# Adding the near half of the position bias to the row-maximum search by matmuls instead of in VectorE's reduction

## The chip, the cores and the metric

The kernel runs on one core of a Trainium2 chip. The metric is the device time of one execution, in microseconds (us). TensorE is called PE below, VectorE DVE, ScalarE ACT, GpSimd POOL, and SyncE, which here only issues DMAs, SP.

## The reference, cut to what matters

Two transformer-like layers run one after the other on an input of 2 x 2048 rows of 256 numbers. The change touches only the first stage, causal attention with 16 heads of 16 columns. For each head, with q and k from one projection of x:

```
s[i, j] = q[i] . k[j] / 16 + bias(i - j)      for j <= i  (rpb: 1023 relative positions)
p       = softmax(s[i, :])
out[i]  = p @ v
```

The bias depends on the distance alone. The table is stored less its last value, so at the distances beyond one end of it there is nothing to add. For a query in tile I, a value is added to the keys of tiles 0 to I - 8 (`FAR = 8`) alone. What matters here: the softmax needs the maximum of each row of s before the exponentials, and so the bias has to be in the scores from which that maximum is taken.

## The kernel before, in words

The whole program is a sequence of phases with a barrier between them. The first one, `phase_attention`, lasts from the start to about 1037 us of the profile; after it come the projection, a mixture of branches, a state-space scan and a mixture of experts, none of which is edited.

A "pair" p is one head for both batch rows b = 0, 1. Batch row 0 lives on partitions 0 to 48 and batch row 1 on 64 to 112 of the arrays `qs` and `ks` (49 rows: one row for the maximum, then 48 rows of high and low parts of q or k). So a matmul of one batch row uses the upper 64 rows of the PE array and one of the other batch row the lower 64.

Attention is a software pipeline over pairs. While pair p is scored, pair p+1 is searched for its row maxima. The loop `for p in range(-1, PAIRS + 1)` on PE has 10 steps (`STEPS`) of 4 slots x (`SLOTS`); p = -1 only searches, next to the last products of the input projection, and the passes for p = 0 to 14 do both. In each slot:

- `score` (L519) computes a piece of transposed scores of pair p, keys on the partitions, up to 512 columns; `add_far` (L535) adds a bias from the tables `far` to those pieces that need it, 12 matmuls of 64x64 tiles for both batch rows. ACT takes the exponential (L619).
- `search` (L506) computes a piece (I, g) of pair p+1, queries of tile I on the partitions, keys of group g (512 columns) along the free side. DVE takes its maximum in `largest`: a plain reduction (L714) where nothing has to be added, an add-and-maximum with a triangular mask on the diagonal (L717), and an add-and-maximum with the bias table `near` where `is_near(I, g)` (L711). An add-and-maximum issues a second instruction that reads the accumulator. 12 of the 40 pieces of a pair are near ones; all 12 stand in even slots, and all are 512 columns wide.
- `sums` (L562), in slots 1 and 3 between the two batch rows, multiplies the probabilities of the step before with v: 8 matmuls.

Three PSUM banks (`RING = 3`) hold the searched pieces and three the scored ones. A search waits until DVE has read the piece three turns before it (`S1_FREE`, semaphore `s1_read`), a score until ACT has read the piece three turns before it (`s2_read`). DVE waits for `s1_ready`.

The maxima go back into the scores as one more row of `qs`: DVE collects them (`collect`), PE transposes them (`turn_max`, L571, in slot 2 of step 0 and of step 7), DVE negates them into `mxT` (L731), and SP stores them with a DMA (`store_max`, L331) into rows 0 and 64 of `qs`. PE waits for that DMA (`mrow_loaded`) at steps 0 and 2 of the pair. POOL, in order, does `cut` (L430, the causal mask on probabilities), `gather_values` (L417) and `round_stack` (L409).

Of the kernel before, what the change touches and what calls it, by code (L numbers as in the profile page):

```python
# [123 lines left out]
REACH = FAR * P  # L124
SPAN = REACH - P + 4 * P
# [68 lines left out]
def is_near(I, g):  # L194

    return (I - FAR + 1) * P > g * CH


def hidden_turns():

    at = sorted(at for turn, at in S1_AT.items() if turn[0] == "max" and (SEARCHED[turn[2]][1] == SEARCHED[turn[2]][0] // TPC or is_near(*SEARCHED[turn[2]])))
    return {a: n % 4 for n, a in enumerate(at)}, {a: at[n - 4] + 1 if n >= 4 else 0 for n, a in enumerate(at)}
# [9 lines left out]
def phase_attention(nc, t):  # L212
# [3 lines left out]
    with nc.cleanup_on_exit(), ExitStack() as ctx:  # L216
# [4 lines left out]
        near = [sp.sb(f"near{s}", [P, SPAN], BF16) for s in range(2)]  # L221
# [5 lines left out]
        mxT = [sp.sb(f"mxT{n}", [2 * HALF, P], F32R) for n in range(2)]  # L227
# [18 lines left out]
        mrow_loaded = [sp.sem(f"mrow_loaded{n}") for n in range(2)]  # L246
        vst_ready = sp.sem("vst_ready")
# [39 lines left out]
        def _(eng):  # L287
# [28 lines left out]
            def load_near(h):  # L316
                if h >= 2:
                    eng.wait_ge(s1_read, last_search(h - 2, 0))
                at = t.tables[1, ds(h, 1), 0:1]
                eng.dma_start(near[h % 2][:, SPAN - REACH:], bass.AP(tensor=at.tensor, offset=at.offset, ap=[[1, P], [1, REACH]])).then_inc(near_loaded[h % 2], 16)  # L320

# [6 lines left out]
            def store_max(p, n):  # L328
                eng.wait_ge(s1_read, S1_AT["row", p, n] + 1)
                for b in range(2):  # L330
                    eng.dma_start(qs[p % 3][b * P // 2:b * P // 2 + 1, n * S // 2:(n + 1) * S // 2].bitcast(F32),  # L331
                                  mxT[n][b * HALF:(b + 1) * HALF, :].bitcast(F32)).then_inc(mrow_loaded[n], 16)
# [62 lines left out]
        def _(eng):  # L395
# [3 lines left out]
            for s in range(2):  # L399
# [3 lines left out]
                step(nc.gpsimd.memset(near[s][:, 0:SPAN - REACH], 0.0))  # L403
# [8 lines left out]
            def gather_values(p):  # L412
# [32 lines left out]
            for n, (kind, u) in enumerate(USES):  # L445
# [4 lines left out]
                if n == len(USES) - 10:  # L450
                    round_stack(1)
            gather_values(0)
            for p in range(PAIRS):
                for step in range(STEPS):
                    if step == 1 and p + 1 < PAIRS:
                        gather_values(p + 1)
                    if step == 3 and p + 2 < PAIRS:
                        round_stack(p + 2)
                    cut(p, step)

        @block.tensor
        def _(eng):
# [35 lines left out]
            eng.wait_ge(pool_set, 11)  # L498

            def search(p, x, b):  # L500

                I, g = SEARCHED[x]
                lo, hi = g * CH, min(g * CH + CH, (I + 1) * P)
                at = S1_AT["max", p, x, b]
                after(eng, s1_read, S1_FREE[at])
                mm = nc.tensor.matmul(s1[:, S1_BANK[at], 0:hi - lo], qs[p % 3][half(b, ROWS), I * P:(I + 1) * P],  # L506
                                      ks[p % 3][half(b, ROWS), lo:hi], start=True, stop=True)
                mm.then_inc(s1_ready, 1)
# [72 lines left out]
            for p in range(-1, PAIRS + 1):  # L581
                if p + 1 < PAIRS:
                    eng.wait_ge(stack_ready, 2 * p + 4)
                for step in range(STEPS):
                    if 0 <= p < PAIRS and step in (0, 2):
                        eng.wait_ge(mrow_loaded[1 - step // 2], 32 * (p + 1))
                        eng.wait_ge(far_loaded[p % 2], 96 * (p // 2 + 1))
                    for x in range(SLOTS):
                        for b in range(2):
# [4 lines left out]
                            if b == 0 and x in (1, 3) and p >= 0:  # L594
                                if step > 0 and p < PAIRS:
                                    sums(p, step - 1, x // 2)
                                if step == 0 and p > 0:
                                    sums(p - 1, STEPS - 1, x // 2)
                        if p == -1 and x % 2 == 1:
# [73 lines left out]
        def _(eng):  # L673
# [27 lines left out]
            def largest(p, x, b):  # L701
# [5 lines left out]
                if is_near(I, g):  # L707
                    begin = SPAN - CH - (TB - 1 - I) * P - g * CH
                    eng.wait_ge(near_loaded[p % 2], 16 * (p // 2 + 1))
                    after(eng, s1_read, HID_FREE[at])  # L710
                    nc.vector.tensor_tensor_reduce(out=hid[HID[at]][:, 0:width], in0=piece, in1=near[p % 2][:, begin:begin + width][:, ::-1], scale=1.0, scalar=-3.0e38,  # L711
# [2250 lines left out]
```

## Time and profile before

| | us |
|---|---|
| median of 3 runs | 2526.55 |
| lowest and highest | 2526.16, 2528.66 |
| profiled execution, its own time | 2526.16 |
| profiled execution, its span from first to last instruction | 2524.2 |
| PE busy over the span | 2377.9 |
| DVE busy | 1928.0 |
| ACT busy | 1434.8 |
| POOL busy | 1045.9 |

The mean granted TensorE clock is 0.981 of full speed. Busy time of PE is to be read with care: matmuls overlap, their ends are modelled, and two matmuls of different row halves of the array can run at once. Better is the distance between starts in the timeline. PE rows of the timeline merge neighbours of one line: "x2" with its start is the start of the first. "PEld" is the loading of weights. In the shapes, "49*128 49x512" is a weight of 49 rows and 128 columns with 512 streamed columns.

### The profile page before, as it was taken

What the parts mean: (1) busy time and instruction counts of PE and PEld (TensorE: products, weight loads), DVE (VectorE), ACT (ScalarE), POOL (GpSimd) and SP (SyncE); (2) the same over time, 40 slices, a digit from 0 to 9 for tenths busy, and PEclk for the clock granted to TensorE, in tenths of its full rate; (3) what the DMA queues carried; (4) which work ended last, traced back from release to release, by engine and by line L of the source; (5) the groups of instructions that cost most, each with busy time, mean ns of one, the idle gap of its engine ahead of it and who ended that gap; (6) DMA issues with size and microseconds to landing.
All of it is one profiled execution on the core that took longest, in us unless ns stands there. A gap on an engine that the chain in (4) does not pass through costs nothing. (4 is left out here: it accounts for less than half of the span.)

```text
span 2524.2 us, 42210 instructions
## 1 busy us (share of the span) xinstructions
PE 2377.9 (94%) x14291; PEld 1515.4 (60%) x14291; DVE 1928.0 (76%) x4358; ACT 1434.8 (57%) x2608; POOL 1045.9 (41%) x1030
## 2 busy tenths in 40 slices
PE   8999999999999999899999997999999999999992
PEld 4433333333333333467777775888888777787782
DVE  3888888888888884266666665999999999898366
ACT  3466666666666667444444454666566686654420
POOL 3511211111121111110000001899999887898464
PEclk9999999999999999999999998999999999999996
DMA  8644433333334421100000000111111122124694
GB/s 252 182 74 73 87 62 61 61 61 61 61 61 74 72 67 70 56 17 17 17 17 17 18 26 30 51 60 54 63 59 56 65 101 84 63 72 142 222 330 158
DMA packets 117325, 200.20 MB, mean 79 GB/s; under 512 B 16644, under 2 KB 75064, under 8 KB 113912
## 3 DMA queue, kind: packets, MB, share of 16 engines
q1 hardware_dynamic: 89880, 160.28, 24.2%
q10 hardware_dynamic: 21088, 20.45, 2.4%
q0 software_dynamic: 6144, 16.79, 2.0%
q8 instruction: 115, 1.88, 0.3%
q14 instruction: 98, 0.80, 0.1%
HBM read 114.18 MB, written 78.79 MB: 76 GB/s over the span
## 5 line engine op out<-in xcount | busy, mean ns | idle before, releaser
L619 ACT ACTIVATE ssm_in_dt<-att_s 128x512 f32<-128x512 f32 (+3 forms) x1280 | 609.9, 535 | 301.6 <-PE att_s L519 176.9
L519 PE MATMUL att_s<-att_qs,att_ks 49*128 49x512 f32 (+3 forms) x1280 | 428.8, 417 | 22.7 <-ACT ssm_in_dt L619 20.3
L519 PEld LDWEIGHTS att_s<-att_qs,att_ks 49*128 49x128 f32 x1280 | 207.5, 185 | 391.5 <-ACT ssm_in_dt L619 324.9
L506 PE MATMUL att_s<-att_ks,att_qs 49*128 49x512 f32 (+3 forms) x1280 | 427.3, 420 | 4.0 <-DVE att_qs L698 4.0
L1932 PE MATMUL ssm_ps<-ssm_hi,ssm_halves 128*128 128x512 f32 x1024 | 407.3, 398 | 14.4 <-DVE ssm_lo L2390 7.1
L1933 PE MATMUL ssm_ps<-ssm_lo,ssm_halves 128*128 128x512 f32 x1024 | 401.4, 392 | 0.0
L1934 PE MATMUL ssm_ps<-ssm_hi,ssm_halves 128*128 128x512 f32 x1024 | 401.2, 392 | 0.0
L430 POOL TENSOR_SCALAR_AFFINE_SELECT ssm_in_dt<-ssm_in_dt 128x256 f32<-128x256 f32 x256 | 104.6, 408 | 673.1 <-ACT ssm_in_dt L619 583.7
L2323 POOL TENSOR_TENSOR ssm_cc<-ssm_cc,ssm_h 128x512 f32<-128x512 f32 x256 | 332.3, 1298 | 75.8 <-DVE ssm_h L2419 67.4
L562 PE MATMUL att_o_ps<-ssm_in_dt,att_vst 128*32 128x512 f32 (+3 forms) x2560 | 340.6, 542 | 5.3 <-ACT ssm_in_dt L619 5.3
L2332 POOL TENSOR_TENSOR ssm_out_z<-ssm_out_z,ssm_cc 128x512 f32<-128x512 f32 x256 | 338.7, 1323 | 0.1
L714 DVE TENSOR_REDUCE att_partmax<-att_s 128x1 f32<-128x512 f32 x384 | 256.1, 686 | 69.5 <-PE att_s L506 67.3
L717 DVE CUSTOM_DVE_ANT_0 att_hid<-att_s,att_hidden 128x512 bf16<-128x512 f32 (+3 forms) x512 | 238.8, 488 | 85.4 <-PE att_s L506 84.5
L2116 ACT ACTIVATE ssm_cc<-ssm_ps,ssm_par 128x512 f32<-128x512 f32 x256 | 198.5, 775 | 156.1 <-PE ssm_ps L1934 155.8
L711 DVE CUSTOM_DVE_ANT_0 att_hid<-att_s,att_near 128x512 bf16<-128x512 f32 x384 | 248.8, 685 | 7.0 <-PE att_s L506 6.6
L2110 ACT ACTIVATE ssm_ps<-ssm_in_dt,ssm_par 128x512 f32<-128x512 f32 x256 | 177.1, 692 | 118.4 <-DVE ssm_h L2419 116.1
L1932 PEld LDWEIGHTS ssm_ps<-ssm_hi,ssm_halves 128*128 128x128 f32 x1024 | 193.7, 189 | 60.7 <-issue 10.2
L2395 DVE SCALAR_TENSOR_TENSOR ssm_inp<-ssm_ps,ssm_par,ssm_in_u 128x512 f32<-128x512 f32 x256 | 190.0, 742 | 41.5 <-PE ssm_ps L1934 41.4
L506 PEld LDWEIGHTS att_s<-att_ks,att_qs 49*128 49x128 f32 x1280 | 203.4, 185 | 27.4 <-DVE att_partmax L717 6.3
L1934 PEld LDWEIGHTS ssm_ps<-ssm_hi,ssm_halves 128*128 128x128 f32 x1024 | 193.9, 189 | 41.5
L1933 PEld LDWEIGHTS ssm_ps<-ssm_lo,ssm_halves 128*128 128x128 f32 x1024 | 193.9, 189 | 40.2 <-issue 1.2
L2419 DVE TENSOR_TENSOR_SCAN ssm_h<-ssm_ps,ssm_h,ssm_inp 128x512 f32<-128x512 f32 x160 | 203.0, 1269 | 0.4
(331 smaller groups left out, 3683.6 us busy)
## 6 DMA issues: line engine op xcount, KB each, us to landing
qk_halves<-ssm_in_dt SPq DMA_DIRECT2D x64, 256.0 KB, 3.0
scan_halves<-ssm_halves SPq DMA_DIRECT2D x32, 512.0 KB, 2.9
ssm_halves<-scan_halves SPq DMA_DIRECT2D x32, 512.0 KB, 3.4
moe_sorted<-att_hidden SPq DMA_DIRECT2D x31, 512.0 KB, 10.2
moe_answers<-ssm_cc ACTq DMA_DIRECT2D x62, 256.0 KB, 3.8
att_far<-bias_tables SPq DMA_DIRECT2D x96, 136.0 KB, 8.6
att_stage_q<-qk_halves SPq DMA_DIRECT2D x96, 128.0 KB, 4.4
att_stage_k<-qk_halves SPq DMA_DIRECT2D x96, 128.0 KB, 5.9
```

Source lines behind the costliest of these rows:

```text
L506: mm = nc.tensor.matmul(s1[:, S1_BANK[at], 0:hi - lo], qs[p % 3][half(b, ROWS), I * P:(I + 1) * P], ks[p % 3][half(b, ROWS), lo:hi], start ...
L519: mm = nc.tensor.matmul(s2[:, turn % RING, 0:hi - lo], ks[p % 3][half(b, ROWS), J * P:(J + 1) * P], qs[p % 3][half(b, ROWS), lo:hi], start ...
L562: mm = nc.tensor.matmul(o_ps[32 * g:32 * g + 32, b, lo:CH], vst[p % 2][b][:, J, :], prob[:, b, step % 2, x * CH + lo:(x + 1) * CH], start= ...
L619: nc.scalar.activation(prob[:, b, step % 2, x * CH + lo:(x + 1) * CH], s2[:, turn % RING, 0:CH - lo], ACT.Exp, scale=1.0 / HD).then_inc(s2 ...
L711: nc.vector.tensor_tensor_reduce(out=hid[HID[at]][:, 0:width], in0=piece, in1=near[p % 2][:, begin:begin + width][:, ::-1], scale=1.0, sca ...
L714: nc.vector.tensor_reduce(most, piece, AX, ALU.max).then_inc(s1_read, 1)
L717: nc.vector.tensor_tensor_reduce(out=hid[HID[at]][:, 0:width], in0=piece, in1=hidden[:, CH - width:CH], scale=1.0, scalar=-3.0e38, op0=ALU ...
L1932: nc.tensor.matmul(out_ps, halves[m][:, 0, k, col], hi[:, slot, k], start=k == 0, stop=False)
L1933: nc.tensor.matmul(out_ps, halves[m][:, 0, k, col], lo[:, slot, k], start=False, stop=False)
L1934: mm = nc.tensor.matmul(out_ps, halves[m][:, 1, k, col], hi[:, slot, k], start=False, stop=k == KT - 1)
L2323: nc.gpsimd.tensor_tensor(at, at, h[:, g % H_RING], ALU.mult).then_inc(multiplied, 1)
L2332: nc.gpsimd.tensor_tensor(part, part, cc[:, g % Y_RING].rearrange("p (s j) -> p s j", s=2), ALU.add).then_inc(y_added, 1)
```

## The change

The near bias is no longer added by DVE. A new PE function `add_near` adds it in PSUM, after both batch rows of the slot were searched and before `add_far`: for each half s of the array's columns of a flip matrix, one matmul per batch row, 4 matmuls per near piece pair. Only the columns that have a bias, `min(hi, (I - 7) * 128) - lo`, are streamed; for the 12 near pieces of a pair and batch row these are 512 (six times), 384, 256 and 128 (twice each): 4608 columns. The semaphore `s1_ready` of such a piece now comes from its last `add_near` matmul. DVE reads the piece with the plain reduction.

The table `near` gets the layout of `far`: two DMAs per head of 64 partitions and 1088 columns, instead of one of 128 partitions and 1024 columns. PE, instead of DVE, waits for them, at the beginning of a pair.

The row of maxima takes another way: `mxT` is stored into a new tile `mrow`, and POOL copies (and rounds) it from there into `qs`, two copies of 1x1024 (`place_max`), in its step 1 (`place_max(p, 0)`) and its step 9 (`place_max(p + 1, 1)`). PE waits for the semaphore `row_ready` of the copies instead of for the DMA.

```diff
-near = [sp.sb(f"near{s}", [P, SPAN], BF16) for s in range(2)]
+mrow = sp.sb("mrow", [P, S])
+near = [sp.sb(f"near{s}", [P, WIN], BF16) for s in range(2)]
...
 def load_near(h):
     if h >= 2:
-        eng.wait_ge(s1_read, last_search(h - 2, 0))
-    at = t.tables[1, ds(h, 1), 0:1]
-    eng.dma_start(near[h % 2][:, SPAN - REACH:], bass.AP(...ap=[[1, P], [1, REACH]])).then_inc(near_loaded[h % 2], 16)
+        eng.wait_ge(s1_ready, last_search(h - 2, 0))
+    for r in range(2):
+        eng.dma_start(near[h % 2][half(r), :], window(0, h)).then_inc(near_loaded[h % 2], 16)
...
 def store_max(p, n):
     eng.wait_ge(s1_read, S1_AT["row", p, n] + 1)
+    after(eng, row_ready, 4 * p if n == 0 else 4 * p - 2)
     for b in range(2):
-        eng.dma_start(qs[p % 3][...].bitcast(F32), mxT[n][...].bitcast(F32)).then_inc(mrow_loaded[n], 16)
+        eng.dma_start(mrow[...], mxT[n][...]).then_inc(mrow_loaded[n], 16)
...
+def place_max(p, n):
+    eng.wait_ge(mrow_loaded[n], 32 * (p + 1))
+    for b in range(2):
+        row, cols = slice(b * P // 2, b * P // 2 + 1), slice(n * S // 2, (n + 1) * S // 2)
+        nc.gpsimd.tensor_copy(qs[p % 3][row, cols], mrow[row, cols]).then_inc(row_ready, 1)
+        eng.wait_ge(row_ready, 4 * p + 3 - 2 * n + b)
...
 def search(p, x, b):
     ...
-    mm = matmul(s1[...], qs[...], ks[...], start=True, stop=True)
-    mm.then_inc(s1_ready, 1)
+    mm = matmul(s1[...], qs[...], ks[...], start=True, stop=not has_near)
+    if not has_near:
+        mm.then_inc(s1_ready, 1)
+
+def add_near(p, x):
+    I, g = SEARCHED[x]
+    lo, hi = g * CH, min(g * CH + CH, (I - FAR + 1) * P)
+    for s in range(2 if hi > lo else 0):
+        at = 15 * P - I * P + lo + s * P // 2
+        for b in (1, 0):
+            mm = nc.tensor.matmul(s1[:, S1_BANK[S1_AT["max", p, x, b]], 0:hi - lo], flip_b[half(b), s],
+                                  near[p % 2][half(b), at:at + hi - lo], start=False, stop=s == 1)
+            if s == 1:
+                mm.then_inc(s1_ready, 1)
...
 for p in range(-1, PAIRS + 1):
     if p + 1 < PAIRS:
         eng.wait_ge(stack_ready, 2 * p + 4)
+        eng.wait_ge(near_loaded[(p + 1) % 2], 32 * ((p + 1) // 2 + 1))
     for step in range(STEPS):
         if 0 <= p < PAIRS and step in (0, 2):
-            eng.wait_ge(mrow_loaded[1 - step // 2], 32 * (p + 1))
+            eng.wait_ge(row_ready, 4 * p + 2 + step)
...
+            if p + 1 < PAIRS:
+                add_near(p + 1, SLOTS * step + x)
...
 # DVE, largest(p, x, b)
-    if is_near(I, g):
-        ...
-        nc.vector.tensor_tensor_reduce(out=hid[...], in0=piece, in1=near[p % 2][...][:, ::-1], ..., op0=ALU.add, op1=ALU.max, accum_out=most)
-    elif g < I // TPC:
+    if g < I // TPC:
         nc.vector.tensor_reduce(most, piece, AX, ALU.max).then_inc(s1_read, 1)
```

On PE, around slot 2 of step 0, before (L519 score, L506 search, L571 the transposition of the maxima, L562 the sums):

```order
L506 MATMUL att_s<-att_ks,att_qs 128x512 [waits att_s1_read]
L571 MATMUL att_s<-att_ident,att_mx 16x128 [waits att_s1_read,att_mx_ready]
L519 MATMUL att_s<-att_qs,att_ks 128x512 [waits att_s2_read]
L506 MATMUL att_s<-att_ks,att_qs 128x512 [waits att_s1_read]
L562 MATMUL att_o_ps<-ssm_in_dt,att_vst 32x128
```

The same place in the changed kernel (its lines are L541 score, L515 search, L527 `add_near`, L593 transposition, L584 sums):

```order
L515 MATMUL att_s<-att_ks,att_qs 128x512 [waits att_s1_read]
L527 MATMUL att_s<-att_near,att_flip_b 128x512 x4
L593 MATMUL att_s<-att_ident,att_mx 16x128 [waits att_s1_read,att_mx_ready]
L541 MATMUL att_s<-att_qs,att_ks 128x512 [waits att_s2_read]
L515 MATMUL att_s<-att_ks,att_qs 128x512 [waits att_s1_read]
L584 MATMUL att_o_ps<-ssm_in_dt,att_vst 32x128
```

Four matmuls stand between the second search of the slot and the transposition. At slot 0 of step 2, where PE now waits for `row_ready` and where a far addition (L535 before, L557 now) stands too, the changed kernel has:

```order
L541 MATMUL att_s<-att_qs,att_ks 128x512 [waits att_s2_read,att_far_loaded1,att_row_ready]
L515 MATMUL att_s<-att_ks,att_qs 128x512 [waits att_s1_read]
L541 MATMUL att_s<-att_qs,att_ks 128x512 [waits att_s2_read]
L515 MATMUL att_s<-att_ks,att_qs 128x512 [waits att_s1_read]
L527 MATMUL att_s<-att_near,att_flip_b 128x128 x4
L557 MATMUL att_s<-att_far,att_flip_b 64x512 x12
L541 MATMUL att_s<-att_qs,att_ks 128x512 [waits att_s2_read]
```

The near additions go ahead of the far ones. On POOL, in the changed kernel (L432 the causal cut, L420 the row copies, L412 the values):

```order
L432 AFFINE_SELECT ssm_in_dt<-ssm_in_dt 128x2x128 [waits att_s2_read,att_cut_done] x8
L420 CAST att_qs<-att_mrow 1x1024 [waits att_mrow_loaded1,att_cut_done]
L420 CAST att_qs<-att_mrow 1x1024 [waits att_row_ready]
L432 AFFINE_SELECT ssm_in_dt<-ssm_in_dt 128x2x128 [waits att_s2_read,att_row_ready]
L432 AFFINE_SELECT ssm_in_dt<-ssm_in_dt 128x2x128 [waits att_s2_read,att_cut_done] x3
L420 CAST att_qs<-att_mrow 1x1024 [waits att_mrow_loaded0,att_cut_done]
L420 CAST att_qs<-att_mrow 1x1024 [waits att_row_ready]
L412 COPY att_vst<-ssm_out_z 128x16x16 [waits att_summed,att_row_ready]
```

Before, the twelve cuts stood in one run, with nothing between them. Each pair of copies now waits behind the cuts ahead of it and holds up what follows.

## Rows read from the trace of the kernel before

**Rows 1.** Busy time in a stretch: PE, PEld, DVE, ACT, POOL, clock, DMA, GB/s

```profile
500.00:560.00 60.00, 57.65 (x492) 22.94 (x490) 49.02 (x153) 40.65 (x86) 11.20 (x21) 1.00 0.32 64
```

**Rows 2.** Timeline of PE, a half step with a far addition: start, length, instructions

```profile
534.41 1.06 PE L562 MATMUL att_o_ps<-ssm_in_dt,att_vst 128*32 128x256 f32 x8
535.41 0.49 PE L519 MATMUL att_s<-att_qs,att_ks 49*128 49x512 f32 x1
...
535.75 0.62 PE L519 MATMUL att_s<-att_qs,att_ks 49*128 49x512 f32 x2
535.98 0.39 PE L506 MATMUL att_s<-att_ks,att_qs 49*128 49x512 f32 x1
536.30 0.84 PE L535 MATMUL att_s<-att_far,att_flip_b 64*64 64x512 bf16 x12
537.07 0.50 PE L519 MATMUL att_s<-att_qs,att_ks 49*128 49x512 f32 x1
...
537.50 1.06 PE L562 MATMUL att_o_ps<-ssm_in_dt,att_vst 128*32 128x128 f32 x8
```

**Rows 3.** Timeline of PE, a half step without a far addition

```profile
500.04 1.06 PE L562 MATMUL att_o_ps<-ssm_in_dt,att_vst 128*32 128x512 f32 x8
...
502.22 0.49 PE L519 MATMUL att_s<-att_qs,att_ks 49*128 49x512 f32 x1 [0.22 <-ACT ssm_in_dt L619]
...
502.77 1.06 PE L562 MATMUL att_o_ps<-ssm_in_dt,att_vst 128*32 128x512 f32 x8
```

**Rows 4.** Timeline of PE, slots 2 and 3 of step 0

```profile
522.72 0.49 PE L506 MATMUL att_s<-att_ks,att_qs 49*128 49x512 f32 x1
523.33 0.27 PE L571 MATMUL att_s<-att_ident,att_mx 128*16 128x128 f32 x1
...
523.85 0.49 PE L506 MATMUL att_s<-att_ks,att_qs 49*128 49x512 f32 x1
524.27 1.06 PE L562 MATMUL att_o_ps<-ssm_in_dt,att_vst 128*32 128x128 f32 x8
```

**Rows 5.** Timeline of DVE at the same place

```profile
523.10 0.69 DVE L711 CUSTOM_DVE_ANT_0 att_hid<-att_s,att_near 128x512 bf16<-128x512 f32 x1
...
523.71 0.69 DVE L711 CUSTOM_DVE_ANT_0 att_hid<-att_s,att_near 128x512 bf16<-128x512 f32 x1
...
525.83 0.69 DVE L714 TENSOR_REDUCE att_partmax<-att_s 128x1 f32<-128x512 f32 x1 [0.64 <-PE att_s L506]
```

**Rows 6.** Timeline of PE, narrower score and search pairs

```profile
570.18 0.43 PE L519 MATMUL att_s<-att_qs,att_ks 49*128 49x256 f32 x2
570.30 0.32 PE L506 MATMUL att_s<-att_ks,att_qs 49*128 49x256 f32 x1
...
575.05 0.38 PE L519 MATMUL att_s<-att_qs,att_ks 49*128 49x128 f32 x2
575.16 0.27 PE L506 MATMUL att_s<-att_ks,att_qs 49*128 49x128 f32 x1
```

**Rows 7.** Timeline of PE in the first pass, which only searches

```profile
89.18 0.73 PE L506 MATMUL att_s<-att_ks,att_qs 49*128 49x512 f32 x4
89.84 1.98 PE L480 MATMUL att_o_ps<-ssm_in_u,ssm_in_dt 128*128 128x512 f32 x4
```

**Rows 8.** Page, part 5: the plain and the near maximum on DVE

```profile
L714 DVE TENSOR_REDUCE att_partmax<-att_s 128x1 f32<-128x512 f32 x384 | 256.1, 686 | 69.5 <-PE att_s L506 67.3
L711 DVE CUSTOM_DVE_ANT_0 att_hid<-att_s,att_near 128x512 bf16<-128x512 f32 x384 | 248.8, 685 | 7.0 <-PE att_s L506 6.6
```

**Rows 9.** Lines of instructions: reading the accumulator on DVE, loading weights on PE

```profile
L535 PEld LDWEIGHTS att_s<-att_far,att_flip_b 64*64 64x64 bf16 x2304 | 48.0, 105 | 75.8 <-issue 64.8
L711 DVE DVE_READ_ACCUMULATOR2_ANT att_partmax<- 128x1 f32 x384 | 31.9, 83 | 0.0
```

**Rows 10.** Timeline of POOL: a cast of 2048 columns

```profile
541.42 1.90 POOL L409 CAST att_qs<-att_stage_q 113x2048 fp32r<-113x2048 f32 x1
```

**Rows 11.** Timeline of SP: the stores of a pair's maxima

```profile
524.62 1.30 SPq L331 DMA_DIRECT2D att_qs<-att_mxT  x2
```

More of the change, by code:

```diff
@@ L191 @@
 S1_BANK, S1_FREE, ALONE = search_banks()
-def is_near(I, g):
-    return (I - FAR + 1) * P > g * CH
 def hidden_turns():
-    at = sorted(at for turn, at in S1_AT.items() if turn[0] == "max" and (SEARCHED[turn[2]][1] == SEARCHED[turn[2]][0] // TPC or is_near(*SEARCHED[turn[2]])))
+    at = sorted(at for turn, at in S1_AT.items() if turn[0] == "max" and SEARCHED[turn[2]][1] == SEARCHED[turn[2]][0] // TPC)
     return {a: n % 4 for n, a in enumerate(at)}, {a: at[n - 4] + 1 if n >= 4 else 0 for n, a in enumerate(at)}
@@ L226, in phase_attention @@
         mx = [sp.sb(f"mx{n}", [P, 2, HALF]) for n in range(2)]
-        mxT = [sp.sb(f"mxT{n}", [2 * HALF, P], F32R) for n in range(2)]
+        mxT = [sp.sb(f"mxT{n}", [2 * HALF, P]) for n in range(2)]
         oT = [sp.sb(f"oT{b}", [P, CH]) for b in range(2)]
@@ L402, in _ @@
                     step(nc.gpsimd.memset(vst[s][b][:, :, HD + 1:32], 0.0))
-                step(nc.gpsimd.memset(near[s][:, 0:SPAN - REACH], 0.0))
             def round_stack(p):
@@ L451, in _ @@
                     round_stack(1)
+                if n == len(USES) - 3:
+                    place_max(0, 1)
             gather_values(0)
@@ L454, in _ @@
                 for step in range(STEPS):
-                    if step == 1 and p + 1 < PAIRS:
-                        gather_values(p + 1)
+                    if step == 1:
+                        place_max(p, 0)
+                        if p + 1 < PAIRS:
+                            gather_values(p + 1)
                     if step == 3 and p + 2 < PAIRS:
                         round_stack(p + 2)
+                    if step == 9 and p + 1 < PAIRS:
+                        place_max(p + 1, 1)
                     cut(p, step)
@@ L506, in search @@
                 mm = nc.tensor.matmul(s1[:, S1_BANK[at], 0:hi - lo], qs[p % 3][half(b, ROWS), I * P:(I + 1) * P],
-                                      ks[p % 3][half(b, ROWS), lo:hi], start=True, stop=True)
-                mm.then_inc(s1_ready, 1)
+                                      ks[p % 3][half(b, ROWS), lo:hi], start=True, stop=not has_near)
+                if not has_near:
[10 more added lines that the diff above has]
+                            mm.then_inc(s1_ready, 1)
             def score(p, step, x, b):
@@ L706, in largest @@
                 piece, most = s1[:, S1_BANK[at], 0:width], partmax[:, b, I, g:g + 1]
-                if is_near(I, g):
[L708 to L711, printed above, removed]
-                                                   op0=ALU.add, op1=ALU.max, accum_out=most).then_inc(s1_read, 1)
-                elif g < I // TPC:
+                if g < I // TPC:
                     nc.vector.tensor_reduce(most, piece, AX, ALU.max).then_inc(s1_read, 1)
```

13 lines of the change are left out of this document (6 added, 7 removed).

## The prediction

> **What bounds the kernel now.** I first asked how far each engine is busy while pairs are searched and scored together. Over a stretch of 60 us in the middle PE is busy for 57.65 of 60 us, DVE for 49.02, ACT for 40.65 and POOL for 11.20, at full granted clock [rows 1]. PE is nearly full, but that number is padded by modelled ends, so I went on to the timeline of PE and took the distances between starts.
>
> In a half step with a far addition (from one `sums` to the next, 534.41 to 537.50, 3.09 us) the pieces follow each other without a recorded wait: `sums` 1.00, the first score and search pair 0.34, the next 0.23, the third 0.32, the far addition 0.77, the last pair 0.43 [rows 2]. That adds up to 3.09. A pair of a score and a search, 512 columns each, costs 0.23 and not twice that; at 2.4 GHz 512 columns alone are 0.213. So the two row halves of the array work at once and PE streams. In this kind of half step whatever is added to PE should be paid in full.
>
> A half step without a far addition lasts 2.73 us (500.04 to 502.77), and there PE has a gap of 0.22 us before a score, waiting for ACT [rows 3]. So there some added work is free. The third kind is slot 2 of step 0: the second search starts at 522.72, the transposition at 523.33, and the search after it only at 523.85, 0.14 after DVE finished with the piece of the near maximum that it had begun at 523.10 (the next begins at 523.71) [rows 4, 5]. There PE is paced by DVE for a moment.
>
> DVE itself waits: 69.5 us in front of the plain maxima and 7.0 in front of the near ones, mostly for searches on PE [rows 8]. It does not set the pace in general.
>
> **What the change takes from DVE.** 384 add-and-maximum operations of 685 ns become 384 plain ones of 686 ns, on equal shapes: 0 [rows 8]. Also 384 accumulator reads of 83 ns go, 31.9 us in all [rows 9], but I cost them at nothing: the near maxima started at 523.10 and 523.71, 0.61 apart, less than the length of one [rows 5], so the reads already lie beside the next operation, and DVE waits for PE anyway. At best that is a gain of 32 us; it returns as a rival below.
>
> **What it adds to PE.** 12 near pieces per pair, each 4 matmuls. The two of one s are for different row halves, as the score and search pair is, so I price two matmuls as one such pair, and a near piece at two of those. A pair costs 0.23 at 512 columns [rows 2], 0.12 at 256 and 0.11 at 128 [rows 6]; for 384 I take 0.17, between. So a near piece costs 0.46, 0.34, 0.24 or 0.22 us. The lower bound is the bare stream, 2 x columns / 2400: 0.43, 0.32, 0.21, 0.11.
>
> Which slots they fall in decides how much is paid. From the table of searches: eight stand in slots with a far addition (512 columns in step 2 slot 2, step 3 slot 2 and step 6 slot 0; 384 in step 5 slot 2; 256 in steps 4 and 5, slot 0; 128 in steps 2 and 3, slot 0), four in slots without one (512 in step 0 slots 0 and 2 and in step 1 slot 2; 384 in step 6 slot 2).
>
> - The eight: 3 x 0.46 + 0.34 + 2 x 0.24 + 2 x 0.22 = 2.64 us per pair from above, 2688 columns x 2 / 2400 = 2.24 from below. I take 2.5, nearer the upper end because the pair price is a measured distance.
> - Slot 2 of step 0: the near matmuls also delay DVE. Its second search starts at 522.72; 0.23 later the first near pair goes, 0.23 later the second, at 523.18. From the start of a search to the maximum that reads it there are 0.56 (the sums of 524.27 last 1.00, so the search after them starts at 525.27, and its maximum at 525.83) [rows 2, 4, 5]. So DVE starts at 523.74 instead of 523.10, and the search that waits for this piece, and the sums after it, move by 0.64. Below, 0, if DVE's lateness is caught up; I take 0.64, since that search waits for it today.
> - The other three: between 0, in the gap, and their full 0.46 + 0.46 + 0.34 = 1.26. The gap is 0.22 where it is recorded and the price 0.46 [rows 3], so I take half, 0.63.
>
> Sum per pair 2.5 + 0.64 + 0.63 = 3.77, between 2.24 and 2.64 + 0.64 + 1.26 = 4.54. Fifteen passes score and search together: 56.6 us (33.6 to 68.1).
>
> The first pass only searches. Four searches start at 89.18, products follow at 89.84 and run on [rows 7]; nothing waits there, so its 12 pieces are paid: 6 x 0.46 + 2 x 0.34 + 2 x 0.24 + 2 x 0.22 = 4.36 from above, 4608 x 2 / 2400 = 3.84 from below; I take 4.1.
>
> The Trainium skill, "TensorE: Matmul & The Clock Gate", in Part 3 (The mechanism), says that a weight load overlaps with running matmuls only where it goes to another row group. The two values of s need different weights in the same row half, so by that rule each of the 384 steps (12 x 2 x 16) would also pay a load. The rows speak against it: successive pairs, whose weights also go to the same two halves, stand 0.23 apart, 0.02 over the bare stream [rows 2]. What an exposed load would make of the time is in a rival.
>
> **What it moves.** The row of maxima takes a detour: store, then two POOL casts of 1024 columns, in order behind POOL's cuts. A cast of 2048 columns takes 1.90 [rows 10], so about 0.95 each, 1.9 together. The two stores are issued from 524.62 to 525.92 [rows 11]. PE needs the result at the first score of step 2; the sums of 534.41 are those of slot 1 of that step, behind three pairs (0.34, 0.23, 0.32) and a far addition (0.77) and one more pair, so that score is at about 532.4. Between lie 6.5 us, of which 1.9 are casts, so the landing may take 4.6. The path of step 7 to step 0 is longer. POOL is busy for only 11.20 of 60 us [rows 1], and the 3.8 per pair fit. Its next jobs, values and a cut, come about 2 us later, still before their sums. I cost it at 0; from the other side it is at worst what the third rival says. On the SP queue one load of `near` becomes two, needed a whole pair later; the row stores keep their place. PE's wait for `near` at the head of a pair costs nothing for the same reason: 0.
>
> **Sum.** 56.6 + 4.1 = 60.7 us, bounds 37.4 and 72.5. The profiled execution took 2526.16, span 2524.2; the median of the runs is 2526.55, 0.4 apart. 2526.2 + 60.7 = 2586.9: 2587 us, 2.4% slower. Its own range is 2563 to 2600.
>
> **Rivals.**
> 1. PE is less full than it seems: its ends are modelled, and the 0.34 and 0.32 of [rows 2] against 0.23 may be waits that near matmuls would fill. Then the four slots without far additions cost nothing and the eight half, 1.25 per pair, and the first pass 2: 15 x 1.25 + 2 = 21 us, 2547. For it: DVE and ACT's idle gaps. Against: the far half step adds up with no recorded wait.
> 2. The near matmuls do not pair up, or their weight loads are exposed. One after the other they cost as much again, 2 x 60.7 = 121 us: 2648. Exposed loads at the nearest row, 105 ns for 64x64 [rows 9], cost 384 x 0.105 = 40 us on top of 60.7: 2627. For it: the trace has no 64x128 bf16 matmul. Against: the 0.23.
> 3. The detour is late at step 2. If a store takes 8 us to land instead of under 4.6, because the next pair's loads are queued right behind it, PE stands 3.4 us per pair, 54 us in all: 2641.
> 4. The other side: DVE sets the pace, through the chain search, maximum, freed bank, search. Then the accumulator reads count, 384 x 0.083 = 32 us less, and PE's additions lie in its waits: 2494. It decides from the point where DVE has no idle time in front of the maxima. Rows 8 show 76.5 us of it, so I give it little.
>
> **How the numbers follow.** Forecast 0.71, rival 1 0.12, rival 2 0.10, rival 3 0.04, rival 4 0.03. The range takes the forecast's own bounds, most of rival 1 and stops short of rival 2's: 2550 to 2620. A change under 0.2% (5 us) can't be told from none here; only a corner of rival 1 lies there, 0.02. Faster is rival 4, 0.03. Slower 0.95.
>
> **What would show it.** PE: `add_near`'s second pair starts 0.21 to 0.24 after the first at 512 columns; half steps like that of [rows 2] last 3.5 instead of 3.09; the row transposition to sums in step 0 grows by about 0.6; the stretch per pair grows by 3.8. DVE: the idle time in front of its maxima grows by some 60 us, while plain maxima keep 686 ns. POOL: casts of 1x1024 near 0.95 us, done 2 us or more before the first score of step 2. The forecast is wrong if near pairs stand 0.4 or more apart, if PE waits for POOL, or if the half steps with far additions do not grow.

## The result, and the profile after

| | before | changed |
|---|---|---|
| median, us | 2527.61 (4 runs, 2526.16 to 2528.67) | 2573.09 (4 runs, 2569.24 to 2574.62) |
| profiled execution, its own time | 2526.16 | 2575.21 |
| its span | 2524.2 | 2573.5 |
| PE busy | 2377.9 | 2437.0 |
| DVE busy | 1928.0 | 1933.2 |
| POOL busy | 1045.9 | 1110.4 |

The changed kernel takes 1.018 times as long (1.0168 to 1.0192): 45.5 us more, where 60.7 was forecast. It is slower as forecast, and inside the range. In the profiled executions the difference is 49.3 us of span, and the accounts below are made against that.

The first view is the stretch of one whole pair, from the sums of step 2, slot 1, to the same sums of the next pair. The columns are those of [rows 1]. In the changed kernel:

```profile
501.93:562.52 60.59, 59.01 (x525) 23.61 (x523) 47.66 (x125) 38.50 (x82) 15.21 (x24) 1.00 0.34 64
```

The same stretch in the kernel before:

```profile
534.41:592.05 57.64, 55.52 (x476) 22.16 (x474) 47.23 (x149) 38.51 (x82) 11.12 (x20) 1.00 0.34 66
```

A pair became 2.95 us longer, at full clock in both. DVE's busy time hardly changed (47.66 against 47.23), although 24 instructions went (the accumulator reads); POOL has 4.1 more (four casts). Fifteen such pairs are 44.3 of the 49.3 us.

Next, PE's timeline in the half step with a far addition that answers to [rows 2]:

```profile
501.93 1.07 PE L584 MATMUL att_o_ps<-ssm_in_dt,att_vst 128*32 128x256 f32 x8
502.92 0.49 PE L541 MATMUL att_s<-att_qs,att_ks 49*128 49x512 f32 x1
...
503.26 0.62 PE L541 MATMUL att_s<-att_qs,att_ks 49*128 49x512 f32 x2
503.49 0.39 PE L515 MATMUL att_s<-att_ks,att_qs 49*128 49x512 f32 x1
503.73 0.61 PE L527 MATMUL att_s<-att_near,att_flip_b 64*128 64x512 bf16 x4
504.26 0.84 PE L557 MATMUL att_s<-att_far,att_flip_b 64*64 64x512 bf16 x12
505.04 0.50 PE L541 MATMUL att_s<-att_qs,att_ks 49*128 49x512 f32 x1
...
505.47 1.06 PE L584 MATMUL att_o_ps<-ssm_in_dt,att_vst 128*32 128x128 f32 x8
```

It lasts 3.54 us (501.93 to 505.47) against 3.09: 0.45 more for a near piece priced at 0.46. The distance to the far addition is larger, 0.53 (503.73 to 504.26), but the last search now has a successor at 0.24 where it had one at 0.32. The half step without a far addition, which answers to [rows 3]:

```profile
527.42 1.06 PE L584 MATMUL att_o_ps<-ssm_in_dt,att_vst 128*32 128x512 f32 x8
...
528.98 0.39 PE L515 MATMUL att_s<-att_ks,att_qs 49*128 49x512 f32 x1
529.22 0.50 PE L527 MATMUL att_s<-att_near,att_flip_b 64*128 64x384 bf16 x4
529.59 0.49 PE L541 MATMUL att_s<-att_qs,att_ks 49*128 49x512 f32 x1
...
530.15 1.07 PE L584 MATMUL att_o_ps<-ssm_in_dt,att_vst 128*32 128x512 f32 x8
```

It lasts 2.73 us (527.42 to 530.15), exactly as before, with a near piece inside whose two matmuls in one row half start 0.17 us apart, so about 0.35 in all. The reader can see how much room there was. The near piece starts 1.80 after the sums (529.22 less 527.42). Before, the last score started 2.18 after them (502.22 less 500.04) [rows 3]. So there were 0.38 us between these two starts, not the 0.22 that is recorded as idle. Even 0.38 is not the limit. In slot 0 of step 0 a piece of 512 columns, which makes the half step above 0.45 longer, stands in the same distance:

```profile
547.44 0.39 PE L515 MATMUL att_s<-att_ks,att_qs 49*128 49x512 f32 x1
547.67 0.61 PE L527 MATMUL att_s<-att_near,att_flip_b 64*128 64x512 bf16 x4
548.05 0.44 PE L541 MATMUL att_s<-att_qs,att_ks 49*128 49x384 f32 x1
```

Its half step (545.87 to 548.55) keeps its 2.68 us too. But a piece that adds nothing to its own half step can add to the next: the half step that follows the 384 columns of step 6 has no near work, and grew from 2.87 to 2.95.

Slots 2 and 3 of step 0, PE, which answer to [rows 4]:

```profile
550.13 0.50 PE L515 MATMUL att_s<-att_ks,att_qs 49*128 49x512 f32 x1
550.29 0.80 PE L527 MATMUL att_s<-att_near,att_flip_b 64*128 64x512 bf16 x4
551.02 0.28 PE L593 MATMUL att_s<-att_ident,att_mx 128*16 128x128 f32 x1
...
551.68 0.50 PE L515 MATMUL att_s<-att_ks,att_qs 49*128 49x512 f32 x1
552.11 1.07 PE L584 MATMUL att_o_ps<-ssm_in_dt,att_vst 128*32 128x128 f32 x8
```

And DVE there, which answers to [rows 5]:

```profile
550.93 1.29 DVE L733 TENSOR_REDUCE att_partmax<-att_s 128x1 f32<-128x512 f32 x2 [0.31 <-PE att_s L527]
```

From the second search of the slot to the sums are 1.98 us (550.13 to 552.11) against 1.55 before (522.72 to 524.27) [rows 4]. DVE starts its maximum 0.80 after that search; before it was 0.38 [rows 4, 5]. It now waits for L527. So the delay runs through DVE as forecast, but is 0.42, not 0.64. There are two reasons. The first stands in the first two rows: the near matmuls start 0.16 us after the search, before its 0.213 us of columns can have passed. They belong to the other batch row, in the other row half, and stream beside it; the second one of that row starts at 550.52, 0.39 after the search and not 0.46. The second reason is the larger one: from there to the maximum are 0.41 us (550.52 to 550.93), where the forecast had put in 0.56, the distance from a search to its maximum.

The first pass of the changed kernel, which answers to [rows 7], and the transpositions of maxima, first those of the changed kernel and then those of before (least, median and greatest length in ns; first and last start):

```profile
86.66 0.49 PE L515 MATMUL att_s<-att_ks,att_qs 49*128 49x512 f32 x2
86.99 0.61 PE L527 MATMUL att_s<-att_near,att_flip_b 64*128 64x512 bf16 x4
87.25 0.58 PE L515 MATMUL att_s<-att_ks,att_qs 49*128 49x512 f32 x2
87.76 1.98 PE L488 MATMUL att_o_ps<-ssm_in_u,ssm_in_dt 128*128 128x512 f32 x4
```

```profile
L593 PE MATMUL att_s<-att_ident,att_mx x32: 269/277/380, 109.3 to 1035.0; 128*16 128x128 f32 x32
```

```profile
L571 PE MATMUL att_s<-att_ident,att_mx x32: 269/269/380, 104.8 to 983.8; 128*16 128x128 f32 x32
```

The first transposition comes 4.5 us later (109.3 against 104.8): the first pass, forecast at 4.1. The last comes 51.2 later. That is 44.3 + 4.5 and 2.4 more, which arise as the first pair begins; there both kernels have a stretch of lower granted clock. The changed kernel, four microseconds with the lowest value and then the 20 us around them:

```profile
128.00:132.00 4.00, 3.96 (x18) 2.09 (x17) 2.66 (x10) 1.92 (x5) 0.00 (x0) 0.50 0.29 76
124.00:144.00 20.00, 19.50 (x127) 8.38 (x131) 12.93 (x32) 11.58 (x24) 6.39 (x12) 0.74 0.67 106
```

In the kernel before, the 20 us that hold its own low stretch:

```profile
120.00:140.00 20.00, 19.95 (x145) 8.25 (x145) 15.52 (x48) 13.13 (x28) 5.10 (x10) 0.83 0.78 120
```

A granted 0.50 is the lower of the clock's two levels, 1.2 GHz. A mean of 0.74 instead of 0.83 over 20 us is an estimated 1.8 of the 2.4 us. It is not in every execution of this kernel: a second profile of the changed kernel, unedited (below, "The changed kernel again"), has 0.83 there, its first transposition comes at 108.9, 4.1 after that of before, and 1.1 us instead of 2.4 are left over:

```profile
124.00:144.00 20.00, 19.81 (x141) 8.16 (x145) 13.65 (x33) 11.71 (x24) 6.58 (x11) 0.83 0.73 112
```

The phases after attention, which are not edited, took 2.0 us less. Together 44.3 + 4.5 + 2.4 - 2.0 = 49.2.

Last, the detour of the maxima in the changed kernel: POOL, SP, and the first score of step 2 on PE:

```profile
554.98 2.12 POOL L420 CAST att_qs<-att_mrow 1x1024 fp32r<-1x1024 f32 x2 [3.93 <-DMA att_mrow<-att_mxT]
```

```profile
552.43 1.30 SPq L327 DMA_DIRECT2D att_mrow<-att_mxT  x2
```

```profile
560.36 0.49 PE L541 MATMUL att_s<-att_qs,att_ks 49*128 49x512 f32 x1
```

POOL waits for the landing, copies until 557.10, and PE needs the row at 560.36: 3.3 us of room. The page's groups of maxima on DVE, which answer to [rows 8]:

```profile
L733 DVE TENSOR_REDUCE att_partmax<-att_s 128x1 f32<-128x512 f32 x768 | 494.2, 686 | 112.8 <-PE att_s L515 66.3
```

The 768 maxima of 512 columns keep 686 ns, and wait 112.8 us where 76.5 (69.5 + 7.0) stood before. The diagonal maxima wait 94.6 where they waited 85.4, so all of them together wait 45.5 longer.

### The profile page after: what moved, and what is told of

It is laid out like the page before. It is cut to its first block and busy times, and to the rows that moved or that the text cites. A ratio compares the mean times of both kernels' runs of the same rounds, so it can differ in the third digit from the quotient of the medians.

```text
span 2573.5 us, 43116 instructions
## 1 busy us (share of the span) xinstructions
PE 2437.0 (95%) x15059; PEld 1542.2 (60%) x15059; DVE 1933.2 (75%) x3974; ACT 1435.0 (56%) x2608; POOL 1110.4 (43%) x1092
## 5 line engine op out<-in xcount | busy, mean ns | idle before, releaser
L733 DVE TENSOR_REDUCE att_partmax<-att_s 128x1 f32<-128x512 f32 x768 | 494.2, 686 | 112.8 <-PE att_s L515 66.3
L541 PE MATMUL att_s<-att_qs,att_ks 49*128 49x512 f32 (+3 forms) x1280 | 435.8, 421 | 16.1 <-ACT ssm_in_dt L644 13.7
L515 PE MATMUL att_s<-att_ks,att_qs 49*128 49x512 f32 (+3 forms) x1280 | 435.9, 426 | 4.4 <-DVE att_qs L723 4.3
L541 PEld LDWEIGHTS att_s<-att_qs,att_ks 49*128 49x128 f32 x1280 | 208.1, 185 | 380.1 <-ACT ssm_in_dt L644 307.3
L432 POOL TENSOR_SCALAR_AFFINE_SELECT ssm_in_dt<-ssm_in_dt 128x256 f32<-128x256 f32 x256 | 104.0, 406 | 622.7 <-ACT ssm_in_dt L644 546.4
L584 PE MATMUL att_o_ps<-ssm_in_dt,att_vst 128*32 128x512 f32 (+3 forms) x2560 | 340.8, 542 | 5.3 <-ACT ssm_in_dt L644 5.3
L736 DVE CUSTOM_DVE_ANT_0 att_hid<-att_s,att_hidden 128x512 bf16<-128x512 f32 (+3 forms) x512 | 238.9, 487 | 94.6 <-PE att_s L515 93.8
L515 PEld LDWEIGHTS att_s<-att_ks,att_qs 49*128 49x128 f32 x1280 | 204.4, 186 | 28.1 <-DVE att_partmax L733 10.4
L2419 DVE SCALAR_TENSOR_TENSOR ssm_inp<-ssm_ps,ssm_inp 128x512 f32<-128x512 f32 x256 | 170.6, 666 | 0.0
```

The source lines that it names most:

```text
L541: mm = nc.tensor.matmul(s2[:, turn % RING, 0:hi - lo], ks[p % 3][half(b, ROWS), J * P:(J + 1) * P], qs[p % 3][half(b, ROWS), lo:hi], start ...
L584: mm = nc.tensor.matmul(o_ps[32 * g:32 * g + 32, b, lo:CH], vst[p % 2][b][:, J, :], prob[:, b, step % 2, x * CH + lo:(x + 1) * CH], start= ...
L733: nc.vector.tensor_reduce(most, piece, AX, ALU.max).then_inc(s1_read, 1)
```

## The experiments

Three chips were used. On the first the kernel before took 2526.89 (17 runs), on the second 2552.8 (7), on the third 2526.49 (7); so times are compared with the kernel before on the same chip, and a time that an expectation gives in us is one of the first chip. The second chip is slower only behind attention: a pair takes 60.55 us there with the four matmuls reordered, and 60.59 in the profile above, while the phases behind attention take 1508 to 1516 us there and 1482 to 1486 on the others. Slots are told as (step, slot). "A pair" below is the stretch of the first view, and the growth of a half step is the mean of eleven pairs.

**The detour undone.** Near matmuls stay, but the maxima are stored into `qs` directly and POOL copies nothing.

```diff
-    eng.dma_start(mrow[...], mxT[n][...]).then_inc(mrow_loaded[n], 16)
+    eng.dma_start(qs[p % 3][...].bitcast(F32), mxT[n][...].bitcast(F32)).then_inc(mrow_loaded[n], 16)
...
-    place_max(p, 0)
...
-    place_max(p + 1, 1)
...
-    eng.wait_ge(row_ready, 4 * p + 2 + step)
+    eng.wait_ge(mrow_loaded[1 - step // 2], 32 * (p + 1))
```

> The changed kernel, with the row of maxima stored straight into qs again and PE waiting for that store; no row copies on POOL. Theory (all of the cost is PE streaming the near matmuls): no difference from the changed kernel, 2573 us, since the copies end about 3 us before PE's first score of step 2. Rival (the detour through POOL stands on PE's path): faster than the changed kernel, by up to 3 us a pair, 2530 to 2565.

Measured 2575.24 us (2572.07 to 2575.92), ratio 1.0189 (1.0175 to 1.0203), against 1.018 of the changed kernel. A pair takes 60.55 us against 60.59. The detour costs nothing that can be seen; the third rival is out.

**The near matmuls undone.** The detour and the plain maxima stay, `add_near` issues nothing. It leaves the near bias out of the maxima.

```diff
-    has_near = min(hi, (I - FAR + 1) * P) > lo
+    has_near = min(hi, (I - FAR + 1) * P) > lo and False
...
-    for s in range(2 if hi > lo else 0):
+    for s in range(2 if hi > lo and False else 0):
```

> The changed kernel without its near matmuls: the near bias is left out of the search, DVE reduces the pieces plainly, the detour of the maxima through POOL stays. Theory: the time of the kernel before, 2527.6 us, within 3. Rival (DVE's lost accumulator reads are a gain that the matmuls hide): 2496 to 2520. Rival (the detour costs): 2535 or more.

Measured 2523.14 (2522.23 to 2526.04, 11 runs), ratio 0.9987 (0.9978 to 0.9996), 3.7 us under the kernel before, where at most 3 were expected. The half step of [rows 2] is back at 3.09 us (535.77 to 538.86):

```profile
535.77 1.06 PE L584 MATMUL att_o_ps<-ssm_in_dt,att_vst 128*32 128x256 f32 x8
...
537.65 0.84 PE L557 MATMUL att_s<-att_far,att_flip_b 64*64 64x512 bf16 x12
...
538.86 1.06 PE L584 MATMUL att_o_ps<-ssm_in_dt,att_vst 128*32 128x128 f32 x8
```

So the matmuls are the whole cost, some 50 us. It also tells on the fourth rival: with all accumulator reads of near pieces gone and nothing added to PE, the gain is 3.7 us and not 32. Even that is not in attention: a pair takes 57.62 us here and 57.64 before, and the last sums start at 1037.2 us in this profile and at 1035.9 in that of before. It lies in the phases after it, which are not edited, and is left open.

**Four slots, and eight slots.** The near matmuls only in the four slots without a far addition, (0,0), (0,2), (1,2), (6,2); then only in the other eight. Each leaves the near bias out of the other pieces' maxima. The edit is one condition in `search` and in `add_near`:

```diff
+    ... and x in (0, 2, 6, 26)
+    ... and x not in (0, 2, 6, 26)
```

> The changed kernel with near matmuls only in the four slots that have no far addition (step 0 slots 0 and 2, step 1 slot 2, step 6 slot 2); elsewhere the near bias is left out. The prediction's term for these slots, 1.27 us a pair, gives 15 x 1.27 + 1.8 in the first pass = 21 us, 2549. The trace of the changed kernel shows only about 0.45 a pair in the half steps next to them: 15 x 0.45 + 1.8 = 9 us, 2536 to 2538. Rival (their cost spills into later half steps, 0.3 more a pair): 2541 to 2543.

> The changed kernel with near matmuls only in the eight slots that have a far addition; in the other four the near bias is left out. Theory (PE streams there, all is paid): 15 x 2.45 + 2.7 in the first pass = 39 us, 2566 to 2568, as the prediction's 2.5. Rival (the two groups overlap or compensate each other): under 2560.

Four slots: 2535.11 (2534.33 to 2539.26), ratio 1.0036 (1.0024 to 1.0048), 12.0 us over the kernel without near matmuls. A pair grows by 0.64 us, of it 0.41 in the half step of (0,2), 0.03 in that of (1,2), nothing in those of (0,0) and (6,2), and 0.20 as spill into the half steps behind (1,2) and (6,2), which have no near work here. The forecast had 1.27. Eight slots: 2562.44 (2562.28 to 2563.68), ratio 1.0142 (1.0126 to 1.0158), 39.3 us over it, 2.36 per pair, where 2.5 was forecast. The half steps grow by 0.44 to 0.50 for a piece of 512 columns, 0.34 for 384, 0.24 and 0.10 for the two of 256, and 0.13 for each of 128. The two groups add up: 12.0 + 39.3 = 51.3, beside 52.1 for all twelve without the detour (2575.24 less 2523.14) and some 49 with it (the ratios 1.018 and 0.9987). Most of the forecast's error is in the four slots.

**The near matmuls twice.** Each pair of a value of s is issued two times, 8 matmuls per piece. It adds the near bias twice to the scores that are searched.

```diff
-    for s in range(2 if hi > lo else 0):
+    for turn in range(4 if hi > lo else 0):
+        s = turn % 2
```

> The changed kernel with every near matmul issued twice (the near bias is added twice in the search). Theory (slots without a far addition hide the first dose in a gap that PE has only once): the second dose is paid nearly in full, 2.5 in the far slots and 1.4 to 1.6 in the other four, 4.0 us a pair, and 4.4 in the first pass: 2573 + 64 = 2637. Rival (these slots have room for more, as PE is not what paces them): as much again as the first dose, 2573 + 47 = 2620.

Measured 2664.07 (2660.19 to 2664.21), ratio 1.0428 (1.0411 to 1.0446), 111.3 us over before. In a far half step:

```profile
526.39 1.07 PE L585 MATMUL att_o_ps<-ssm_in_dt,att_vst 128*32 128x256 f32 x8
...
528.19 1.04 PE L528 MATMUL att_s<-att_near,att_flip_b 64*128 64x512 bf16 x8
529.16 0.84 PE L558 MATMUL att_s<-att_far,att_flip_b 64*64 64x512 bf16 x12
...
530.36 1.07 PE L585 MATMUL att_o_ps<-ssm_in_dt,att_vst 128*32 128x128 f32 x8
```

The expectation of 2637 is a ratio of 1.043, and held. The second dose adds 0.43 here (3.97 against 3.54). Eight matmuls of 512 columns pass in 0.97 us; one after another at 2.4 GHz they would take 1.71. Per pair the second dose costs 3.81 where the first cost 2.95. The difference is in the slots without a far addition, which pay some 1.6 for the second dose after 0.64 for the first. Their room is used once.

**The order of the four matmuls.** Both values of s for one batch row, then both for the other.

```diff
-    for s in range(2 if hi > lo else 0):
-        at = 15 * P - I * P + lo + s * P // 2
-        for b in (1, 0):
+    for b in ((1, 0) if hi > lo else ()):
+        for s in range(2):
+            at = 15 * P - I * P + lo + s * P // 2
```

> The changed kernel with the four near matmuls of a piece ordered by batch row first (both column halves of row b = 1, then both of b = 0), so that only the middle two can run side by side. Theory (two row halves of the array at once): three streams instead of two, 0.21 to 0.23 more for 512 columns, 1.2 us more a pair in the far slots and 0.2 to 0.7 in the others, 1.9 in the first pass: 2596 to 2604. Rival (near matmuls never ran side by side): 2573, as before the reordering.

Measured 2601.91 (2599.36 to 2603.7) on the second chip, ratio 1.0187 (1.017 to 1.0204). The expectation was wrong: it is a ratio of 1.027 to 1.030 (2596 to 2604 on the first chip; the 2601.91 is of the second), and the order makes no difference. The half step is 3.54 us again:

```profile
500.39 1.06 PE L584 MATMUL att_o_ps<-ssm_in_dt,att_vst 128*32 128x256 f32 x8
...
502.19 0.61 PE L527 MATMUL att_s<-att_near,att_flip_b 64*128 64x512 bf16 x4
502.73 0.84 PE L557 MATMUL att_s<-att_far,att_flip_b 64*64 64x512 bf16 x12
...
503.93 1.06 PE L584 MATMUL att_o_ps<-ssm_in_dt,att_vst 128*32 128x128 f32 x8
```

Either the four matmuls are not side by side at all and each is cheaper than thought, or each row half works through its own matmuls whatever stands between them. The starts inside the piece, which the view shows in a narrow window, already say the second: two begin at 502.19, though the second in the program is for the same row half as the first.

```profile
502.19 0.39 PE L527 MATMUL att_s<-att_near,att_flip_b 64*128 64x512 bf16 x2
```

The other two begin at 502.42. So the third of the program started beside the first, and before the second. Two more experiments, below, ask the same of the time.

**Narrow near matmuls.** At most 128 columns each, in the same count; it leaves out the near bias of the other columns in the search.

```diff
-    lo, hi = g * CH, min(g * CH + CH, (I - FAR + 1) * P)
+    lo, hi = g * CH, min(g * CH + P, (I - FAR + 1) * P)
```

> The changed kernel with every near matmul cut to 128 columns; the near bias is left out beyond them. Theory (the cost is streamed columns): 0.11 to 0.22 a piece in the far slots, 0.9 to 1.8 us a pair, 0.1 to 0.2 in the others, 2 in the first pass: 2523 + 18 to 32 = 2541 to 2555. Rival (the cost is the weight loads and the instructions, which are the same in number): above 2565.

Measured 2576.21 (2569.72 to 2582.63) on the second chip, ratio 1.0081 (1.0062 to 1.0099), 23.4 us over before. Its four runs are 13 us apart, so this is a rough number; a pair takes 58.80 us, 1.16 over before.

```profile
502.38 0.29 PE L527 MATMUL att_s<-att_near,att_flip_b 64*128 64x128 bf16 x4
502.60 0.52 PE L557 MATMUL att_s<-att_far,att_flip_b 64*64 64x256 bf16 x12
```

From the first near matmul to the far addition are 0.22 us, as priced, over 0.11 of bare columns. But the half step around it grew by only 0.13 (500.58 to 503.36, 2.78 against 2.65): a part of the 0.22 stood between the last search and the far addition before, too. In one row half the second near matmul starts 0.07 us after the first, where its columns take 0.053. So the cost goes with the columns even here.

**Near pieces moved out of slots with far additions.** In the table of searches (11,0) changes places with (12,3), and (14,0) with (14,1): two pieces with 512 near columns go to slots without a far addition, one with 384 comes back.

```diff
-            (12, 3), (13, 3), (13, 0), (12, 2),
-            (8, 0), (15, 3), (14, 0), (14, 2),
+            (11, 0), (13, 3), (13, 0), (12, 2),
+            (8, 0), (15, 3), (14, 1), (14, 2),
...
-            (11, 0), (8, 1), (14, 1), (10, 1),
+            (12, 3), (8, 1), (14, 0), (10, 1),
```

> The changed kernel with four search pieces exchanged: near piece (11, 0), 512 near columns, moves from step 6 slot 0, which has a far addition, to step 1 slot 0, which has none, and (12, 3) takes its place; near pieces (14, 0), 512, and (14, 1), 384, change places between step 2 slot 2 (far addition) and step 6 slot 2 (none). Theory: 0.45 + 0.08 us a pair less paid, nothing new in step 1, where PE waits 0.5 us for ACT: 2573 - 8 = 2565. Rival (DVE's maxima in step 1 come late and hold the freed banks): 2573 or more.

Measured 2588.56 (2587.78 to 2590.01) on the second chip, ratio 1.0138 (1.0121 to 1.0155): 35.8 us over before, 10 less than the changed kernel has on its chip. A pair takes 59.98 us, 0.61 less. The half step of step 6, slot 0, fell from 3.54 to 2.97, below the 3.10 of before. Not all of that is near work: the piece that came, (12,3), is searched with 128 columns where (11,0) has 512. It is the best version with all near matmuls, and still slower than the kernel before, so nothing here beats that.

**The changed kernel again, and near matmuls for one batch row only.** The first is the changed kernel without an edit, on the third chip. The second leaves the near bias out of the search of batch row 1.

```diff
-    for b in (1, 0):
+    for b in (0,):
```

> The changed kernel, unedited, to stand beside the next two on the same chip. Both theories: 1.018 of the kernel before.

> The changed kernel with the near matmuls of batch row b = 0 alone (two a piece instead of four); the near bias of b = 1 is left out. Theory (the two batch rows' matmuls stream side by side in the two row halves): the removed ones cost nothing, 0 to 8 us less than the changed kernel, some of it because the maxima of b = 1 start earlier. Rival (they stream one after the other and the pairing is only in the records): half of the 48 us goes, 22 to 26 us less.

Changed again: 2571.47 (2569.98 to 2575.2), ratio 1.018 (1.0163 to 1.0197). One row: 2569.12 (2566.94 to 2569.67), ratio 1.0167 (1.015 to 1.0184), 2.4 us less for half of the matmuls. The half step with a far addition shows why:

```profile
561.72 1.07 PE L584 MATMUL att_o_ps<-ssm_in_dt,att_vst 128*32 128x256 f32 x8
...
563.53 0.60 PE L527 MATMUL att_s<-att_near,att_flip_b 64*128 64x512 bf16 x2
564.06 0.84 PE L557 MATMUL att_s<-att_far,att_flip_b 64*64 64x512 bf16 x12
...
565.27 1.07 PE L584 MATMUL att_o_ps<-ssm_in_dt,att_vst 128*32 128x128 f32 x8
```

It lasts 3.55 us with two matmuls as with four. That is the direct proof that the two batch rows stream side by side: the second is free there. The 2.4 us themselves understate what one row saves. A pair takes 59.97 us against 60.55, 0.58 less (8.7 in fifteen). It is saved in three half steps: 0.40 in that of (0,2), and 0.11 and 0.08 in those behind (1,2) and (6,2), the same places and sizes as in the four slots above. Against it stands a longer stretch of low clock as the first pair begins, 0.57 over 20 us where the changed kernel again has 0.83, an estimated 5 us:

```profile
124.00:144.00 20.00, 18.71 (x83) 7.05 (x83) 10.63 (x27) 9.54 (x20) 5.81 (x11) 0.57 0.66 97
```

The mean clock of all four executions is lower too, 0.979 to 0.980 against 0.981 to 0.983. Why is not shown. Slots 2 and 3 of step 0 with one row:

```profile
549.81 0.50 PE L515 MATMUL att_s<-att_ks,att_qs 49*128 49x512 f32 x1
550.16 0.60 PE L527 MATMUL att_s<-att_near,att_flip_b 64*128 64x512 bf16 x2
...
551.41 1.06 PE L584 MATMUL att_o_ps<-ssm_in_dt,att_vst 128*32 128x128 f32 x8
```

Two matmuls take the 0.60 that four took. From the search to the sums are 1.60 us here (1.98 with both rows, 1.55 before). So the 0.41 that this slot lost came from batch row 1, whose maximum DVE takes first and which frees the bank for slot 3. It is not the price of streaming: batch row 0 still has its two matmuls there. The 0.20 of spill is gone as well.

**Twice, by batch row.** Eight matmuls as above, first four of batch row 1, then four of batch row 0.

```diff
-    for s in range(2 if hi > lo else 0):
-        for b in (1, 0):
+    for b in ((1, 0) if hi > lo else ()):
+        for turn in range(4):
+            s = turn % 2
```

> Every near matmul twice, as in the earlier doubled kernel, but ordered by batch row: four of b = 1, then four of b = 0 (the near bias is added twice in the search). Theory A (each row half works through its own matmuls and does not wait for the other half's in program order): the time of the doubled kernel, 1.043 of the kernel before. Theory B (starts keep program order): four streams of b = 1, and of b = 0 only the first beside the last of them, 7 streams instead of 4, 0.64 us more for a piece of 512 columns, about 5 us a pair, 1.07 of the kernel before.

Measured 2630.14 (2629.49 to 2634.12), ratio 1.0415 (1.0398 to 1.0433), against 1.0428 for eight in the paired order; a pair takes 64.37 us against 64.40, and the far half step 3.97 in both. Even four matmuls of one half in a row do not hold up the other half.

## Why the prediction was right, and where its sizes were off

- **PE bounds, far slots are paid in full: right.** Forecast 2.5 us per pair, measured 2.36 with the eight slots alone. The half step of [rows 2] was to last 3.5 and lasts 3.54. Only the 256 columns of step 5 came at less than their columns, 0.10, and the pieces of 128 were priced too high, 0.22 for 0.13. The first rival, which had the eight half hidden, is wrong there. It also said that the other four cost nothing, and for three of them that is nearer than the forecast.
- **Two row halves at once: right.** The whole piece adds 0.45, one batch row alone costs as much as both in a far half step, a second dose adds 0.43. The second rival needed twice this, or 0.1 us per weight load; neither is there. By the rule of the Trainium skill ("TensorE: Matmul & The Clock Gate", Part 3, The mechanism) that a load overlaps running matmuls only in another row group, the change of weights within a row half would have shown. The second dose, two more changes of weights in each half, cost 0.43 us where the columns alone take 2 x 0.213, which leaves no room for it. The same section also lets a load into the background weight buffer run ahead, which would fit; no run tells the two apart.
- **Slot 2 of step 0: right in kind, 0.41 instead of 0.64.** Two steps failed. One is "0.23 later the first near pair goes, 0.23 later the second": the near matmuls of batch row 1 do not wait for the search of batch row 0, and its second one started 0.39 after that search. The other is the 0.56 from there to the maximum, read off a search; behind a near matmul it is 0.41. The experiment with one batch row shows that this delay is the slot's whole cost.
- **"The other three": mis-sized, 0.63 instead of 0.23.** This is about half of the error: 0.40 x 15 = 6 us (slot 2 of step 0 is 0.23 x 15 = 3.5, the far slots 0.14 x 15 = 2.1). The step was "The gap is 0.22 where it is recorded and the price 0.46, so I take half". Read by distances between starts the gap was 0.38, and pieces of 0.35 and of 0.45 both passed in it without making their half step longer. The range had 0 as its lower bound, which was nearer. Of what was paid, 0.03 in the half step of (1,2) and 0.20 behind, the 0.20 goes away with the near matmuls of batch row 1 while those of row 0 stream on. So it is not streaming; that it comes by way of later maxima, as in (0,2), was not traced. That the room holds one dose and not two is shown by the doubled kernel.
- **First pass: right.** 4.5 in this profile, 0.1 above its upper bound of 4.36, and 4.1, as forecast, in the second profile of the same kernel.
- **The detour: right, 0.** The casts are longer than forecast, 1.03 instead of 0.95 each (a row of 1024 columns on one partition took no less per column than one on 113), and the room is 3.3 us.
- **DVE's part: right, 0.** Plain maxima are as long as the near ones were, and the reads lay beside other work; without near matmuls the kernel gains 3.7 us and not 32. DVE's idle time was to grow by 60 us, the forecast's whole cost. It grew by 36 in front of the plain and near maxima and by 9 in front of the diagonal ones, 45.5 in all, most of the 51 by which attention got longer: DVE has the same work in more time. The fourth rival's chain (search, maximum, freed bank, search) exists, but only (0,2) shows it, where it is what costs.
- **What was not in the sum:** 2.4 us more at the start of the first pair, an estimated 1.8 of them by the lower clock and not seen again in the second profile, and 2.0 less in later phases. They nearly cancel, and that is luck.

## What to carry to other kernels

Work that moves from an engine with idle time to the one that has none is paid at its full streaming price, however cheap it looks there. Recorded idle time tells too little of what would be free: it was 0.22 where the starts left 0.38, and a piece that costs 0.45 elsewhere passed there. Leaving a part of the work out, as with the four and the eight slots, measured it. Look one half step further, too: work that is free where it stands made the half step behind it up to 0.11 longer. And put such work where the busy engine waits for another: the same matmuls in other slots cost 10 us less.

## What the hardware showed that was not expected

Matmuls that use different row halves of the array do not wait for each other in the order of the program. Of four matmuls in the order of halves 1, 1, 0, 0 the third started beside the first, at 502.19, and the half step took the same 3.54 us as with 1, 0, 1, 0; eight in the order 1, 1, 1, 1, 0, 0, 0, 0 gave 1.0415 beside 1.0428, and 3.97 us for the half step in both. Leaving out the matmuls of one half changed no half step with a far addition (3.55 beside 3.54). Successive near matmuls in one half, each with other weights, started 0.22 to 0.23 us apart at 512 columns, over a bare stream of 0.213, and 0.07 apart at 128, over 0.053.
